# Gated linear recurrence and mixture of experts on one core: recurrences in eight halves through PSUM, and a re-ordered front

## The chip, the cores and the metric

The kernel runs on one core of a Trainium2 chip. The metric is the device time of one execution in microseconds (us). The engines are PE (TensorE, matrix products), DVE (VectorE), ACT (ScalarE), POOL (GpSimd) and SP (SyncE, which here only issues DMAs). They run side by side, each through its own list of instructions in order, and wait for one another on semaphores.

## The reference

```
xn = layernorm(x)                                  # x: 16 x 256 tokens of 128 columns
# branch 1: gated linear recurrence
xc = causal depthwise conv(xn, 4 taps) + conv_b
r, i = sigmoid(xc @ W_r.T + b_r), sigmoid(xc @ W_i.T + b_i)
a = sigmoid(log_a) ** (8 r)
h[t] = a[t] * h[t-1] + sqrt(clip(1 - a*a)) * i * xc        # along the 256 tokens of a sequence
attn = rmsnorm(h @ W_out.T) * gamma
# branch 2: mixture of 8 experts, one expert a token, 512 places an expert
e = argmax(xn @ Wr);  rank = place of the token in its expert's queue;  keep = rank < 512
y[token] = keep * p[token] * relu(xn[token] @ W1[e]) @ W2[e]
out = x + attn + y
```

## The kernel before, in words

The 4096 tokens are 32 tiles of 128 rows. Columns (transposed data) are handled in 8 halves of 512 tokens (`HT`, `NH` = 8) or 4 chunks of 1024 (`TC`, `C` = 4). A sequence is `L` = 256 tokens, so a half holds two sequences and a chunk four. The order on every engine is written by hand.

**The front.** x comes in five units (`UNITS`: 4, 4, 8, 8, 8 tiles), units 0, 2 and 4 on SP's queue and 1 and 3 on ACT's. PE transposes x by halves (`tp`, into dec), ACT copies it out (`untile`), PE computes the router's logits (`router`). DVE takes the mean and variance of each unit (`moments`), ACT the square root (`root`), DVE the reciprocal (`inverse`), and then ACT and POOL write half of the normalised tiles each (`normalise`), which SP stores to `xn_rows` in DRAM. DVE then finds each token's expert and rank in two parts (`marks`, `places`, h = 0 and 1). PE helps with running counts (`counts`) and turns the one-hot products `low_eq` and `hi_val` into a table of the tokens of each expert's places (`table_of`). DVE writes that as `idx_in` and `idx_out` (semaphore `idx_done`).

**Gathers and scatters.** From `idx_done` on, POOL issues 64 indirect DMAs, 128 rows each: for each expert 4 gathers of its tokens from `xn_rows` and 4 scatters of its results to `y_rows`. Gathers run four experts ahead. The program on POOL is gathers of experts 0 to 3, then scatter(0), gather(4), scatter(1), gather(5), ... scatter(7). scatter(e) waits until DVE has copied expert e's results out of PSUM (`evict(e)`, semaphore `y_done`).

**The experts.** For expert e PE transposes the gathered rows (`turn`), ACT copies them (`columns`, xg_hi) and DVE writes the rest (`columns_rest`, xg_lo), PE multiplies with W1 in three passes (`up`, into `hbank`), ACT applies relu (`relu`), PE multiplies with W2 (`down`, into `tb`), DVE evicts (`evict`). ACT and DVE split the next weights (`lead` writes w_hi, `weights_rest` w_lo).

**The recurrence in the experts' gaps.** The tables `PE_AT`, `ACT_AT`, `DVE_AT`, `DVE_LATE`, ... say which stages of branch 1 an engine does at expert e: `AT` before evict (DVE), relu(e+1) (ACT) or up(e+1) (PE), `AFTER` and `LATE` behind them. The first two halves of the convolution are done on PE with diagonal matrices (`conv`, `biased`), the rest on DVE (`taps`). `gates` are the two gate products with tanh. `decay` writes a, `scale` the square root, `recur(c)` multiplies inp by sca and scans chunk c, `project(n)` multiplies half n with W_out into one of three `obank`s, `squares(n)` sums its squares on ACT, `rows(n)` normalises it on DVE and adds it to x.

**The end.** When all scatters have landed, SP reads `y_rows` back in eight DMAs, DVE and ACT weigh the rows by `prob` and add x_tok, and SP and ACT store the result.

## Time and profile before

| | |
|---|---|
| median of 3 runs | 140.11 us (139.97 to 140.36) |
| profiled execution, its own time | 140.53 us |
| its span, first to last instruction | 138.7 us |
| PE busy | 106.6 us (77%) |
| DVE busy | 102.7 us (74%) |
| ACT busy | 92.9 us (67%) |
| POOL busy | 88.0 us (63%) |
| granted TensorE clock, mean | 0.927 |

The span is what the trace shows; 1.8 us of the execution lie around it. A busy share is a mean over stages: the front (to 29 us), the experts (to 121 us) and the end have different limits, so each is read by itself.

### The profile page before, as it was taken

What the parts mean: (1) busy time and instruction counts of PE and PEld (TensorE: products, weight loads), DVE (VectorE), ACT (ScalarE), POOL (GpSimd) and SP (SyncE); (2) the same over time, 40 slices, a digit from 0 to 9 for tenths busy, and PEclk for the clock granted to TensorE, in tenths of its full rate; (3) what the DMA queues carried; (4) which work ended last, traced back from release to release, by engine and by line L of the source; (5) the groups of instructions that cost most, each with busy time, mean ns of one, the idle gap of its engine ahead of it and who ended that gap; (6) DMA issues with size and microseconds to landing.
All of it is one profiled execution on the core that took longest, in us unless ns stands there. A gap on an engine that the chain in (4) does not pass through costs nothing.

```text
span 138.7 us, 2167 instructions
## 1 busy us (share of the span) xinstructions
PE 106.6 (77%) x693; PEld 90.0 (65%) x693; DVE 102.7 (74%) x238; ACT 92.9 (67%) x210; POOL 88.0 (63%) x104
## 2 busy tenths in 40 slices
PE   5789876899999999999999199999999996000000
PEld 5788774764468889779789078889798895000000
DVE  7447789848999999986531199999982969914770
ACT  2368963579578689789699948389497696403650
POOL 8936649048778778787877777898777775700000
PEclk9999999999999999999999968999999999955555
DMA  3995973793355264321613511111110111149995
GB/s 87 313 264 104 371 282 135 239 369 96 57 196 156 71 210 93 152 61 38 208 38 67 197 43 39 37 35 37 41 61 27 52 59 38 38 109 287 329 330 171
DMA packets 14346, 19.20 MB, mean 138 GB/s; under 512 B 1673, under 2 KB 10121, under 8 KB 14336
## 3 DMA queue, kind: packets, MB, share of 16 engines
q1 hardware_dynamic: 8464, 12.91, 29.8%
q0 software_dynamic: 2048, 4.13, 10.0%
q10 hardware_dynamic: 3824, 2.04, 5.5%
q8 instruction: 5, 0.08, 0.2%
q14 instruction: 5, 0.04, 0.1%
HBM read 10.76 MB, written 8.39 MB: 138 GB/s over the span
## 4 chain that ended last, share of the span: by engine, by line
PE 40%; DVE 19%; ACT 16%; DMA 11%; issue 6%; SPq 1%; POOL 1%; POOLq 1%; ACTq 0%; DVEq 0%
PE bank L579 8%; PE bank L566 5%; ACT sq L733 5%; PE bank L568 5%; PE bank L567 5%; DMA dec<-y_rows 4%; DMA x_tok<-in_x 4%; PE bank L499 4%; DVE xnT L990 3%; PE bank L521 3%; PE bank L513 2%; PE bank L523 2%; PE bank L522 2%; DVE stats L803 2%; ACT xn_tok L634 2%
## 5 line engine op out<-in xcount | busy, mean ns | idle before, releaser
L380 POOL DMA_INDIRECT xn_tok<-xn_rows,idx_in x32 | 36.9, 1153 | 14.9 <-issue 14.9
L387 POOL DMA_INDIRECT y_rows<-xn_tok,idx_out x32 | 34.6, 1081 | 10.8 <-issue 9.4
L579 PE MATMUL bank<-w_raw,h_sb 128*128 128x128 f32 x256 | 29.9, 275 | 0.0
L579 PEld LDWEIGHTS bank<-w_raw,h_sb 128*128 128x128 f32 x256 | 29.2, 192 | 0.0
L720 ACT ACTIVATE h_sb<-bank 128x512 f32<-128x512 f32 x32 | 19.2, 599 | 10.5 <-PE bank L568 8.7
L566 PE MATMUL bank<-xg_hi,w_hi 128*128 128x512 f32 x32 | 13.5, 422 | 3.5 <-DVE xg_lo L962 3.5
L568 PE MATMUL bank<-xg_hi,w_lo 128*128 128x512 f32 x32 | 13.2, 413 | 0.0
L567 PE MATMUL bank<-xg_lo,w_hi 128*128 128x512 f32 x32 | 13.1, 408 | 0.0
L356 POOL TENSOR_SCALAR xn_tok<-x_tok,rstd,nmr 128x128 f32<-128x128 f32 x16 | 8.7, 554 | 6.9 <-DVE nmr L813 6.9
L962 DVE TENSOR_TENSOR xg_lo<-bank,xg_hi 128x512 fp32r<-128x512 f32 x8 | 5.5, 687 | 9.7 <-ACT xg_hi L714 9.6
L955 DVE SCALAR_TENSOR_TENSOR xc<-xnT,par,xc 128x1020 f32<-128x1020 f32 (+2 forms) x9 | 11.5, 1278 | 0.3
L765 ACT ACTIVATE dec<-dec,prob 128x128 f32<-128x128 f32 x16 | 5.1, 390 | 8.9 <-DMA dec<-y_rows 8.9
L566 PEld LDWEIGHTS bank<-xg_hi,w_hi 128*128 128x128 f32 x32 | 6.3, 196 | 6.4 <-DVE xg_lo L962 5.1
L733 ACT ACTIVATE sq<-bank 128x128 f32<-128x128 f32 x32 | 8.8, 274 | 2.0 <-PE bank L593 1.2
L990 DVE TENSOR_TENSOR_SCAN xnT<-dec,inp 128x256 f32<-128x256 f32 x16 | 9.7, 667 | 0.0
L419 PE MATMUL bank<-w_router,dec 128*128 128x128 f32 x64 | 8.8, 280 | 0.9 <-ACT dec L639 0.9
L1012 DVE SCALAR_TENSOR_TENSOR sca<-bank,rms,gam 128x128 f32<-128x128 f32 x32 | 9.0, 345 | 0.3
L419 PEld LDWEIGHTS bank<-w_router,dec 128*128 128x128 f32 x64 | 7.8, 191 | 1.5 <-ACT dec L639 1.4
L593 PE MATMUL bank<-par,xnT 128*128 128x128 f32 x64 | 8.3, 275 | 0.0
L593 PEld LDWEIGHTS bank<-par,xnT 128*128 128x128 f32 x64 | 7.9, 192 | 0.2
L695 ACT ACTIVATE dec<-bank,half_b 128x512 f32<-128x512 f32 x8 | 5.5, 688 | 3.6 <-PE bank L523 3.1
L643 ACT ACTIVATE xnT<-bank 128x512 f32<-128x512 f32 x8 | 4.3, 601 | 4.7 <-PE bank L477 4.6
(129 smaller groups left out, 230.4 us busy)
## 6 DMA issues: line engine op xcount, KB each, us to landing
w_raw<-in_weights SPq DMA_DIRECT2D x8, 512.0 KB, 3.7
y_rows<-sca SPq DMA_DIRECT2D x4, 512.0 KB, 6.2
dec<-y_rows SPq DMA_DIRECT2D x8, 256.0 KB, 5.6
xn_rows<-xn_tok SPq DMA_DIRECT2D x3, 512.0 KB, 3.8
x_tok<-in_x SPq DMA_DIRECT2D x2, 512.0 KB, 7.5
out<-dec SPq DMA_DIRECT2D x4, 256.0 KB, 3.7
out<-dec ACTq DMA_DIRECT2D x4, 256.0 KB, 3.5
x_tok<-in_x ACTq DMA_DIRECT2D x1, 512.0 KB, 9.1
```

The lines of the kernel that those rows point to most:

```text
L380: g.indirect_dma_start(gathered[:, s * D:(s + 1) * D], None, xn_rows, bass.IndirectOffsetOnAxis(ap=idx_in[:, s:s + 1], axis=0)).then_inc(g ...
L387: g.indirect_dma_start(y_rows, bass.IndirectOffsetOnAxis(ap=idx_out[:, s:s + 1], axis=0), gathered[:, s * D:(s + 1) * D], None, bounds_che ...
L419: last = mm((bank[6], bank[2])[t // PT][:, o:o + D], xT[:, t * P:(t + 1) * P], w_router[:, :], start=True, stop=True)
L566: mm(b, w_hi[:, e % 2, w], xg_hi[:, :], start=True, stop=False)
L567: mm(b, w_hi[:, e % 2, w], xg_lo[:, :], start=False, stop=False)
L568: mm(b, w_lo[:, e % 2, w], xg_hi[:, :], start=False, stop=True).then_inc(h_mm, 1)
L579: last = mm(tile_of(e, s), h_sb[:, k * CAP + s * P:k * CAP + (s + 1) * P], w_raw[:, e, F + k * D:F + (k + 1) * D], start=(k == 0), stop=(k ...
L593: last = mm(obank[n % 3][:, i * D:(i + 1) * D], hs[:, t * P:(t + 1) * P], par[:, WO_T:WO_T + D], start=True, stop=True)
L720: a(h_sb[:, k * CAP:(k + 1) * CAP], hbank[n % 3][:, :], ACT.Relu).then_inc(h_done, 1)
L733: a(sq[:, :], obank[n % 3][:, i * D:(i + 1) * D], ACT.Square, accum_out=ssq[:, t:t + 1]).then_inc(ssq_done, 1)
L955: ins = v.scalar_tensor_tensor(dst[:, :, back:], src[:, :, 0:L - back], par[:, k:k + 1], dst[:, :, back:], ALU.mult, ALU.add)
L990: last = v.tensor_tensor_scan(hs[:, o:o + L], dec[:, o:o + L], inp[:, o:o + L], 0.0, ALU.mult, ALU.add)
```

## The change

It does these things:

1. x comes in on SP's queue alone, in the order of the units. DVE's `moments(1)` and `moments(2)` move ahead of `inverse(0)` and `inverse(2)`. ACT does `root(1)` ahead of `normalise(0)` and `untile(7)` ahead of `root(4)`. POOL writes the diagonal matrices ahead of `normalise(4)`.
2. PE does three transposes of normalised halves before the counts instead of two, and cuts the convolution of half 0 into pieces between `counts(1)` and the tables. Banks: `conv_bank` is bank 1 and 3, `xn_bank` has three banks.
3. DVE's first convolution (`taps_of_chunk(1)`) and the split of the gate weights move ahead of the probability (now a function `probability`).
4. `recur` works on halves, n = 0 to 7. Its product goes to an `obank` in PSUM (`IN_OBANK`) and the scan reads it there. Each product waits for the scan before it. `rows` writes its product back into the `obank` in place, and the sum reads it there.
5. `scale`, `recur`, `rows` and `lead` move in the tables; `evict(7)` comes ahead of rows 4. Expert 6 is put into two banks and evicted in two pieces, on which its scatters wait separately. `project(2)` now waits for recur 5, and `project(4)` for recur 7, since the scans use their banks.

```diff
-        conv_bank = [bank[7], bank[3]]
-        xn_bank = [bank[4], bank[5], bank[0], bank[1]]
+        conv_bank = [bank[1], bank[3]]
+        xn_bank = [bank[4], bank[5], bank[0]]
+        IN_OBANK = (1, 2, 2, 2, 2, 2, 1, 1)
+        SPLIT_K = ((E - 2) * KF + 2) % 3
+            if e == E - 2 and s < ST // 2:
+                return hbank[SPLIT_K][:, s * D:(s + 1) * D]
...
-        ACT_AT = {0: "decay0 gates1", 1: "gates2", 2: "gates3", 3: "scale1", 7: "squares6 squares7"}
-        ACT_AFTER = {0: "decay1", 1: "decay2", 2: "decay3 scale0", 3: "scale2 scale3", 4: "squares0 squares1",
-                     5: "squares2 squares3", 6: "squares4 squares5"}
-        DVE_AT = {0: "gated0 clip0", 1: "gated1", 2: "clip2", 3: "clip3"}
+        ACT_AT = {0: "decay0 gates1", 1: "gates2", 2: "gates3", 3: "scale0", 4: "scale2", 5: "scale3",
+                  7: "squares6 squares7"}
+        ACT_AFTER = {0: "lead2 decay1", 1: "lead3 decay2", 2: "lead4 decay3", 3: "lead5 scale1", 4: "lead6 squares0 squares1",
+                     5: "lead7 squares2 squares3", 6: "squares4 squares5"}
+        DVE_AT = {0: "gated0 clip0", 1: "gated1", 2: "clip2", 3: "clip3", 4: "recur2", 5: "recur5"}
-        DVE_LATE = {0: "taps3 split2", 1: "split3 clip1 gated2", 2: "gated3", 3: "recur0 recur1", 4: "recur2 recur3", 5: "rows0 rows1",
-                    6: "rows2 rows3 rows4", 7: "rows5 rows6 rows7"}
+        DVE_LATE = {0: "taps3 split2", 1: "split3 clip1 gated2", 2: "gated3", 3: "recur0 recur1",
+                    4: "recur3 recur4", 5: "rows0 rows1 recur6 recur7", 6: "rows2 rows3", 7: "rows4 rows5 rows6 rows7"}
...
-                if u not in ACT_UNITS:
-                    sp.dma_start(tiles(x_tok, t0, nt), tile_rows(x_rows, t0, nt)).then_inc(x_in[u], 16)
+                sp.dma_start(tiles(x_tok, t0, nt), tile_rows(x_rows, t0, nt)).then_inc(x_in[u], 16)
...
             def scatter(e):
                 for s in range(e * ST, (e + 1) * ST):
-                    pool.wait_ge(y_done, s + 1 if e == E - 1 else ST * (e + 1))
+                    if e == E - 1:
+                        pool.wait_ge(y_done, s + 1)
+                    elif e == E - 2:
+                        pool.wait_ge(y_done, (s // 2 + 1) * 2)
+                    else:
+                        pool.wait_ge(y_done, ST * (e + 1))
...
-            columns_of(0)
-            columns_of(1)
-            table_of(0)
+            for n in range(3):
+                columns_of(n)
+            conv(0, 0, 2)
             counts(1)
...
-            for n in range(2, 6):
+            table_of(0)
+            columns_of(3)
+            conv(0, 2, 3)
+            table_of(1)
+            conv(0, 3, TAPS)
+            for n in range(4, NH):
                 columns_of(n)
-            table_of(1)
-            columns_of(6)
-            columns_of(7)
-            conv(0, 0, TAPS)
             conv(1, 0, TAPS)
...
+                    if e == E - 1 and n % 3 == SPLIT_K:
+                        pe.wait_ge(y_done, ST * (E - 2) + ST // 2)
...
             def project(n):
-                pe.wait_ge(scan_done, n // 2 + 1)
+                pe.wait_ge(scan_done, {2: 6, 4: 8}.get(n, n + 1))
                 if n >= 3:
-                    pe.wait_ge(attn_done, 4 * (n - 2))
+                    pe.wait_ge(sum_done, n - 2)
...
             root(0)
             untile(0)
             untile(1)
+            root(1)
             normalise(0)
-            root(1)
...
-            for n in range(NH):
+            for n in range(4):
                 keep_columns(n)
...
             lead(0)
+            for n in range(4, NH):
+                keep_columns(n)
...
-            def recur(c):
-                dve.wait_ge(scale_done, c + 1)
-                dve.wait_ge(gated_done, c + 1)
-                for half in halves(c):
-                    v.tensor_tensor(inp[:, half], inp[:, half], sca[:, half], ALU.mult).then_inc(input_done, 1)
-                for s in range(SC):
-                    o = c * TC + s * L
-                    dve.wait_ge(input_done, 2 * c + 1 + s // 2)
-                    last = v.tensor_tensor_scan(hs[:, o:o + L], dec[:, o:o + L], inp[:, o:o + L], 0.0,
+            def recur(n):
+                cols = slice(n * HT, (n + 1) * HT)
+                given = obank[IN_OBANK[n]][:, :]
+                dve.wait_ge(scale_done, n // 2 + 1)
+                dve.wait_ge(gated_done, n // 2 + 1)
+                if n >= 1:
+                    dve.wait_ge(scan_done, n)
+                if n == 6:
+                    dve.wait_ge(sum_done, 2)
+                v.tensor_tensor(given, inp[:, cols], sca[:, cols], ALU.mult).then_inc(input_done, 1)
+                dve.wait_ge(input_done, n + 1)
+                for s in range(HT // L):
+                    o = n * HT + s * L
+                    last = v.tensor_tensor_scan(hs[:, o:o + L], dec[:, o:o + L], given[:, s * L:(s + 1) * L], 0.0,
                                                 ALU.mult, ALU.add)
...
-                    v.scalar_tensor_tensor(attn[:, t * D:(t + 1) * D], obank[n % 3][:, i * D:(i + 1) * D],
-                                           rms[:, t:t + 1], gam[:, :], ALU.mult, ALU.mult).then_inc(attn_done, 1)
+                    o = obank[n % 3][:, i * D:(i + 1) * D]
+                    v.scalar_tensor_tensor(o, o, rms[:, t:t + 1], gam[:, :], ALU.mult, ALU.mult).then_inc(attn_done, 1)
...
-                v.tensor_tensor(x_tok[:, cols], x_tok[:, cols], attn[:, cols], ALU.add).then_inc(sum_done, 1)
+                v.tensor_tensor(x_tok[:, cols], x_tok[:, cols], obank[n % 3][:, :], ALU.add).then_inc(sum_done, 1)
...
             dve.wait_ge(xnT_done, 4)
             taps_of_chunk(1)
+            split_gates()
+            probability()
             columns_rest(0)
             weights_rest(1)
-            split_gates()
             split(1)
```

How the rows stand on three engines. First PE, at the end of the router (L442 / L448 is `table_of`, L477 / L483 the transposes of normalised halves, L497 and L499 / L503 and L505 the convolution's taps, of which each half has four; L427 to L535 / L433 to L541 are counts). Before:

```order
L442 MATMUL bank<-hi_val,low_eq 128x32 x16
L427 MATMUL bank<-offset,ones 128x128
L429 MATMUL bank<-run,ones 128x128
L432 MATMUL bank<-onehot,later 128x128
L434 MATMUL bank<-run,ones 128x128
L535 MATMUL bank<-run,ones 128x8 x2
L477 MATMUL bank<-ident,xn_tok 128x128 x16
L442 MATMUL bank<-hi_val,low_eq 128x32 x16
L477 MATMUL bank<-ident,xn_tok 128x128 x8
L497 MATMUL bank<-xnT,diag 128x512
L499 MATMUL bank<-xnT,diag 128x2x255
L499 MATMUL bank<-xnT,diag 128x2x254
```

and of the change:

```order
L503 MATMUL bank<-xnT,diag 128x512
L505 MATMUL bank<-xnT,diag 128x2x255
L433 MATMUL bank<-offset,ones 128x128
L435 MATMUL bank<-run,ones 128x128
L438 MATMUL bank<-onehot,later 128x128
L440 MATMUL bank<-run,ones 128x128
L541 MATMUL bank<-run,ones 128x8 x2
L448 MATMUL bank<-hi_val,low_eq 128x32 x16
L483 MATMUL bank<-ident,xn_tok 128x128 x4
L505 MATMUL bank<-xnT,diag 128x2x254
L448 MATMUL bank<-hi_val,low_eq 128x32 x16
L505 MATMUL bank<-xnT,diag 128x2x253
```

The first two taps of half 0 now stand ahead of the counts, the third ahead of the second `table_of` and the fourth behind it; the transposes of the last four halves follow there.

DVE at experts 4 and 5 (L962 is `columns_rest`, L997 / L1002 `evict`, L986 / L991 the product of `recur` and L990 / L995 its scans, L928 / L937 `weights_rest`, L1008 / L1020 the start of `rows`). Before, from `columns_rest` of expert 5 on:

```order
L962 TENSOR_TENSOR xg_lo<-bank,xg_hi 128x512
L997 COPY xn_tok<-bank 128x512
L986 TENSOR_TENSOR inp<-inp,sca 128x512 x2
L990 SCALAR_TENSOR_TENSOR xnT<-dec,inp 128x256 x4
L986 TENSOR_TENSOR inp<-inp,sca 128x512 x2
L990 SCALAR_TENSOR_TENSOR xnT<-dec,inp 128x256 x4
L928 TENSOR_TENSOR w_lo<-w_raw,w_hi 128x512
L962 TENSOR_TENSOR xg_lo<-bank,xg_hi 128x512
L997 COPY xn_tok<-bank 128x512
L1008 RECIPROCAL rms<-rms 128x4
```

and of the change, from the same instruction:

```order
L962 TENSOR_TENSOR xg_lo<-bank,xg_hi 128x512
L991 TENSOR_TENSOR bank<-inp,sca 128x512
L995 SCALAR_TENSOR_TENSOR xnT<-dec,bank 128x256 x2
L1002 COPY xn_tok<-bank 128x512
L991 TENSOR_TENSOR bank<-inp,sca 128x512
L995 SCALAR_TENSOR_TENSOR xnT<-dec,bank 128x256 x2
L991 TENSOR_TENSOR bank<-inp,sca 128x512
L995 SCALAR_TENSOR_TENSOR xnT<-dec,bank 128x256 x2
L937 TENSOR_TENSOR w_lo<-w_raw,w_hi 128x512
L962 TENSOR_TENSOR xg_lo<-bank,xg_hi 128x512
L991 TENSOR_TENSOR bank<-inp,sca 128x512
L995 SCALAR_TENSOR_TENSOR xnT<-dec,bank 128x256 x2
```

Where four scans followed two products, now two scans follow one, with the product in a bank; one half stands ahead of each evict.

ACT around expert 4 (L725 / L735 is `scale` and its table load, L714 / L724 `columns`, L720 / L730 `relu`, L673 / L681 `lead`, L708 and L710 / L718 and L720 `decay`). Before, from the relu of expert 3 on:

```order
L720 ACTIVATE h_sb<-bank 128x512 x4
L673 ACTIVATE w_hi<-w_raw 128x512
L708 ACTIVATE dec<-dec,lna 128x1024
L710 ACTIVATE sca<-dec 128x1024
L725 ACT_TABLE_LOAD
L725 ACTIVATE sca<-sca,eps 128x1024
L714 ACTIVATE xg_hi<-bank 128x512
L725 ACTIVATE sca<-sca,eps 128x1024
L720 ACTIVATE h_sb<-bank 128x512 x4
L673 ACTIVATE w_hi<-w_raw 128x512
```

and of the change:

```order
L730 ACTIVATE h_sb<-bank 128x512 x4
L681 ACTIVATE w_hi<-w_raw 128x512
L718 ACTIVATE dec<-dec,lna 128x1024
L720 ACTIVATE sca<-dec 128x1024
L724 ACTIVATE xg_hi<-bank 128x512
L735 ACT_TABLE_LOAD
L735 ACTIVATE sca<-sca,eps 128x1024
L730 ACTIVATE h_sb<-bank 128x512 x4
L681 ACTIVATE w_hi<-w_raw 128x512
L735 ACTIVATE sca<-sca,eps 128x1024
L724 ACTIVATE xg_hi<-bank 128x512
```

`columns` of expert 4 now stands ahead of the table load and of all scales, and the other scales stand one by one between the later stages.

## Rows read from the trace of the kernel before

**Rows 1.** The page's first part: busy time by engine.
```profile
PE 106.6 (77%) x693; PEld 90.0 (65%) x693; DVE 102.7 (74%) x238; ACT 92.9 (67%) x210; POOL 88.0 (63%) x104
```
**Rows 2.** Timeline of POOL: start, length, line, operands, idle before.
```profile
29.44 1.17 POOL L380 DMA_INDIRECT xn_tok<-xn_rows,idx_in  x1 [5.49 <-issue]
...
86.43 1.40 POOL L387 DMA_INDIRECT y_rows<-xn_tok,idx_out  x1 [0.30 <-issue]
...
115.94 0.97 POOL L387 DMA_INDIRECT y_rows<-xn_tok,idx_out  x1 [1.32 <-DVE xn_tok L1002]
...
120.16 0.97 POOL L387 DMA_INDIRECT y_rows<-xn_tok,idx_out  x1 [0.30 <-issue]
```
**Rows 3.** POOL's busy time by stretch (instructions in brackets), clock, DMA.
```profile
82.00:98.00 16.00, 13.37 (x9) 0.92 0.13 37
98.00:115.00 17.00, 12.85 (x13) 1.00 0.16 49
```
**Rows 4.** Timeline of DVE, the last stage.
```profile
114.89 0.88 DVE L1002 COPY xn_tok<-bank 128x128 f32<-128x128 f32 x4
...
121.13 0.69 DVE L1016 TENSOR_TENSOR x_tok<-x_tok,sca 128x512 f32<-128x512 f32 x1
125.50 1.14 DVE L1065 SCALAR_TENSOR_TENSOR dec<-dec,prob,x_tok 128x128 f32<-128x128 f32 x4 [3.68 <-DMA dec<-y_rows]
```
**Rows 5.** The chain that ended last, merged: start, length, what.
```profile
26.83 1.44 PE bank L442 x16
...
29.15 0.86 PE bank L497 x2
...
36.84 0.63 PE bank L553 x4
...
76.14 1.28 ACT L725
...
78.58 0.49 ACT xg_hi L714
...
92.98 0.62 ACT w_hi L673
...
97.17 0.49 ACT xg_hi L714
...
98.43 0.50 PE bank L566
```
**Rows 6.** Timeline of PE: the second unit's wait, then expert 4.
```profile
7.40 0.66 PE L455 MATMUL bank<-ident,x_tok 128*128 128x128 f32 x4 [1.19 <-DMA x_tok<-in_x]
...
79.85 0.50 PE L566 MATMUL bank<-xg_hi,w_hi 128*128 128x512 f32 x1 [3.08 <-DVE xg_lo L962]
...
81.59 0.63 PE L566 MATMUL bank<-xg_hi,w_hi 128*128 128x512 f32 x1
```
**Rows 7.** Stretches of the x load: per engine, clock, DMA share, GB/s.
```profile
3.50:4.50 1.00, 1.00 (x7) 1.00 (x6) 0.06 (x1) 0.26 (x1) 1.00 (x1) 1.00 1.13 346
7.50:8.50 1.00, 1.00 (x10) 1.00 (x11) 0.65 (x2) 0.40 (x1) 0.30 (x1) 1.00 1.21 290
```
**Rows 8.** Timeline of DVE in the front.
```profile
14.88 0.29 DVE L844 TENSOR_REDUCE top<-bank 128x16 f32<-128x128 f32 x1
...
28.38 0.19 DVE L910 TENSOR_SCALAR idx_in<-bank 128x32 int32<-128x32 f32 x1 [0.21 <-PE bank L442]
```
**Rows 9.** Groups by line and form: busy, mean ns of one, idle before.
```profile
L566 PE MATMUL bank<-xg_hi,w_hi 128*128 128x512 f32 x32 | 13.5, 422 | 3.5 <-DVE xg_lo L962 3.5
L990 DVE TENSOR_TENSOR_SCAN xnT<-dec,inp 128x256 f32<-128x256 f32 x16 | 9.7, 667 | 0.0
L1012 DVE SCALAR_TENSOR_TENSOR sca<-bank,rms,gam 128x128 f32<-128x128 f32 x32 | 9.0, 345 | 0.3
L962 DVE TENSOR_TENSOR xg_lo<-bank,xg_hi 128x512 fp32r<-128x512 f32 x8 | 5.5, 687 | 9.7 <-ACT xg_hi L714 9.6
L986 DVE TENSOR_TENSOR inp<-inp,sca 128x512 f32<-128x512 f32 x8 | 5.1, 677 | 0.0
```

73 lines of the change are left out of this document (37 added, 36 removed).

## The prediction

> **What bounds the kernel now.** I read the busy times first [rows 1]. No engine is over 77% busy, so a mean share says little, and I went on to each engine's timeline. POOL's shows that from the first gather at 29.44 to the last scatter at 120.16 it issues 64 indirect DMAs one behind the other, with 0.30 between them. Its only other wait is at the 61st, the first scatter of expert 7, which stood 1.32 idle until DVE had evicted a tile [rows 2]. Of those 1.32 the usual 0.30 go off, so POOL waited 1.0 for the others and is otherwise its own bound. Its issues aren't equally long: nine of them between 82 and 98 take 13.37, which is 1.49 each; thirteen between 98 and 115 take 12.85, which is 0.99 each [rows 3]. In the slow stretch DVE does its 16 scans and 8 products of the recurrence, all of them with two inputs in SBUF; the issue at 86.43 fell wholly into scans and took 1.40 [rows 2, 9].
>
> The end hangs on POOL. Its last issue ends at 121.13; the first read-back reaches DVE at 125.50, 4.37 later, after DVE had idled 3.68 [rows 2, 4]. DVE's own last normalised row ended at 121.82 [rows 4]. So the end is bound by POOL, and DVE is 3.7 behind it as the next bound. From 125.50 to the end of the span are 13.2, which the change leaves alone.
>
> PE is the second lane. It starts the first `turn` at 36.84 [rows 5], is then full to expert 3, and stands 3.08 before `up(4)` at 79.85 [rows 6], because ACT did a table load at 76.14 and a scale ahead of xg_hi at 78.58 [rows 5]. Behind that wait TensorE fell to the lower clock level (a matmul of 0.63 in `up(4)`, where the mean of its line over all experts is 0.42) [rows 6, 9]; the stretch's granted clock is 0.92 in the mean [rows 3], a mix of the 2.4 and the 1.2 GHz level.
>
> **The front: 1.5 earlier.** The second unit of x lets PE go on at 7.40 [rows 6]. With one queue nearly alone the DMAs moved 346 GB/s, with both 290 [rows 7]. In the order of the units, 0.52 MB must be in before unit 1 is, which at 0.35 MB a us is 1.5 us of transfer, and unit 0 by itself let DVE begin about 4.6. So unit 1 is there at about 5.4 and PE goes on at 6.1, behind its own earlier work. From there I followed ACT's list, since each of DVE's `inverse` waits for a `root` on it: `marks(0)`, at 14.88 before [rows 8], comes at about 13.2, 1.7 earlier. From `marks(0)` to `idx_in` at 28.38 [rows 8] DVE has the same instructions, so all of it moves by 1.7, unless PE is late for the last table. A tap on PE takes 0.86 [rows 5], so the two early ones 1.7. They start once ACT has copied half 0, at 19.9, and end at 21.6, ahead of `counts(1)`, which needs a one-hot at 22.0: hidden. The first table (1.3, of the length of the second's 1.44 [rows 5]), four transposes, 0.44, and the third tap, 0.86, then stand ahead of the last table, which PE reaches at 25.5 where DVE would have let it begin at 26.83 − 1.7 = 25.1 [rows 5]. That costs 0.2 to 0.4 and leaves **1.5 for POOL's start**. SP's stores are all shifted with the tiles and stay hidden; POOL's diagonal matrices, 1.65, fit into its wait before `normalise(4)`.
>
> `turn(0)` at 36.84 [rows 5] needs the first four gathers. The four taps (3.4) taken out of the stretch ahead of it, less two transposed halves (0.9) put in, make PE ready at about 34.2, so it waits for the gathers, which come 1.5 earlier, at about 35.3. But DVE's taps, two SBUF inputs again, now run beside the first four gathers instead of the fifth to eighth. One issue among those got longer by 0.7; I charge 0.3 to both lanes: **PE 1.2 earlier**, POOL 1.2 net. From `turn(0)` on PE is full and keeps that.
>
> **The recurrence on POOL's lane.** The excess in the slow stretch is 9 x (1.49 − 0.99) = 4.5 [rows 3]. DVE's two-SBUF work in it is 16 scans (9.7 in all) and 8 products (5.1), 93% of the 16 us. With the product in PSUM, the scans have one SBUF input, and only the products stay: 8 x 0.68 = 5.4 of 16, 34% [rows 9]. In proportion 4.5 x (1 − 34/93) = 2.9 of the excess goes. Bounds: 0, if scans don't hold POOL up, and 4.5. The Trainium skill's page "SBUF — State Buffer" (Who interferes with whom) says that a DVE instruction with two SBUF inputs holds up a GpSimd instruction that reads SBUF, and one with at most one SBUF input doesn't; by it alone all of the scans' share would go, which is this term.
>
> The 1.0 wait at the 61st issue goes if expert 7 is evicted in time (below). POOL's lane: 121.13 − 1.2 − 2.9 − 1.0 = 116.0, and the read-back is on DVE at **120.4**.
>
> **The recurrence on DVE's, ACT's and PE's lanes.** Each half cost DVE (9.7 + 5.1)/8 = 1.85 before. Now the product drains (0.68), the scan starts behind a wait, and the second scan drains too (0.61 + 0.67): about 2.0. PSUM in place of SBUF I take at nothing: a product with one PSUM input takes 687 ns, with two in SBUF 677 [rows 9]. DVE never writes PSUM in this trace, and no scan reads it. Bounds: a little less than nothing (−0.01), and the fixed part once again, +0.23 an instruction (from 345 ns at 128 columns and 677 at 512, 0.865 a column and 0.234 fixed [rows 9]); the nearest row, 687, says nothing. The Trainium skill, "VectorE: DVE Perf Modes" (The TRN2 errata), gives PSUM sources 62 cycles more than SBUF, 65 ns by its clock; by it the path would be about 1.9 longer (29 instructions, below), an estimate from that page, where the rows show 10 ns.
>
> In times of before (the shift of 1.2 taken off last):
> - ACT: xg_hi of expert 4 moves ahead of the table load and scale, from 78.58 to 76.1 [rows 5]. DVE's part follows, `up(4)` starts at 77.4, not 79.85; it waits 0.3 for the relu behind the scale. Without the long wait I take the upper clock level. PE is at `turn(5)` at 80.5, `down(4)` to 84.5, project 0, `up(5)` 85.4 to 88.2: 4.1 ahead of before.
> - ACT then does lead6 and two `squares`. Before, these stood between 92.98 and 97.17 [rows 5]; now from 88.8 to 92.9. So xg_hi(6) is at 93.4, 4.1 ahead. DVE, with recur 0 to 4 done at 91.0, idles 1.8 for it, then writes xg_lo (94.1) and does recur 5, to 96.1. `project(2)` has waited for that since 93.1, **PE stands 3.0 again**, and `up(6)` starts at 97.0 against 98.43 [rows 5]. So 2.7 of the 4.1 are given back here.
> - DVE: evict(5) 96.8, rows 0 and 1 100.7 (one is a reciprocal, four products of 9.0/32 = 0.28 and a sum of 0.69: 1.97 with their waits [rows 4, 9]), recur 6 and 7 to 104.7, w_lo, and xg_lo(7) at 106.0. PE: `up(6)` to 99.8, turn, down(6) 104.7, project 4 (waits for recur 7) 105.6, `up(7)` 106.05 to 108.8, project 5 109.7, `down(7)` in four tiles 110.6 to 113.3. Expert 7's first eviction ends about 111.0, the last at 113.6, where the four stood from 114.89 on [rows 4].
> - rows 4 to 7 follow, 4 x 1.97: 121.5. Less the shift of 1.2, DVE is free at **120.3**.
>
> POOL's 61st issue would be due at 115.94 − 1.0 − 1.2 − 2.9 = 110.8, and the tile is evicted at 111.0 − 1.2 = 109.8: the wait goes, with 1.0 to spare. Both lanes end together: first read-back used at 120.4, against 125.50, **5.1 earlier**. Profiled: 140.53 − 5.1 = 135.4; its time is 0.42 over the median of the runs, so for these 140.11 − 5.1 = **135.0**.
>
> **The rivals.**
> - The clock falls behind the 3.0 stand at 93 as it did behind 3.08 at 76.8. The row of 0.63 is 0.2 over the mean of 0.42, with 8 of its 12 steps slow: about 1.6 for `up(6)`. PE's lane moves 1.6, DVE's end by 1.1 (the rest is in its idle time), POOL's not: 136.1. For it: the same length of wait. Chance 0.13.
> - Collisions stay: POOL's excess comes from the products or the descriptors, not the scans. POOL ends 2.9 later: 137.9. For it: issues beside the taps are mostly 1.0, though those have two SBUF inputs too. Against it: the issue wholly inside scans. Chance 0.12.
> - The front gives nothing, since PE's third tap and transposes and ACT's copies delay the tables by as much as the load gains, or one queue is no faster while the parameters share the engines. The 1.2 to 1.5 go: 136.4. Chance 0.07.
> - A premium for PSUM: a DVE instruction that reads or writes PSUM where SBUF stood takes a third of the fixed part more, 0.07. On DVE's path to the end are recur 5 to 7 (9 instructions) and rows 4 to 7 (5 each): 29, so 2.0 more, 137.0. Against it: 687 for 677 [rows 9]. Chance 0.06. The Trainium skill's page on VectorE, cited above, comes out close to this, an estimate.
> - Slower than before: the same mechanism at the upper bound. At 0.18 each the 5.1 are gone, at 0.23 it is 6.7 more, 141.7; it decides from 0.18 on. For it: no row has a DVE write to PSUM. Chance 0.05.
> - Better: all of the excess gone (4.5); then DVE's lane still holds 120.3, less at most 0.15 for each of its three late halves, 134.5: inside the first case.
>
> **How the numbers follow.** The forecast holds 0.50, with its own range from 133.0 to 136.0 (the front's 0.3 and POOL's lane by its bounds). The rivals are 0.13, 0.12, 0.07, 0.06 and 0.05, and 0.07 are two of them at once (0.02 still faster, 0.03 the same, 0.02 slower). From 133.0 to 138.0 lie the forecast and the first four rivals, with their tails cut 0.8. A measurement of this kernel tells about 0.3% (0.4 us) from no change. Faster 0.90, same 0.03, slower 0.07.
>
> **What would show it.** `idx_in` at 26.9 (27.2 or later: front wrong). POOL's first issue at 27.9; in the stretch of the recurrences a mean issue of about 1.15, not 1.49; no wait of POOL at its 61st. `up(4)` with a wait under 1; a wait of about 3 on PE before project 2, for DVE's fifth recurrence. Products of 0.68 and scans of 0.67 with PSUM operands. DVE's last row ending at 120 to 121, and an idle time before the first final instruction below 0.5 instead of 3.68. The forecast is wrong above all if the PSUM forms are longer, or if POOL's issues stay at 1.49.

## The result: 5.8 to 7.2 us faster, and the profile after

| | before | after |
|---|---|---|
| median of the runs (four each, side by side) | 140.07 us | 134.28 us (132.64, 133.29, 135.27, 135.62) |
| ratio of the undisturbed runs, 95% interval | | 0.949 [0.9445, 0.9533] |
| profiled execution, its own time | 140.53 | 132.64 |
| its span | 138.7 | 130.8 |

The ratio leaves out two of the four executions of the changed kernel (135.27 and 135.62), which are over 1.5% behind the fastest and had a lower granted clock, 0.937 and 0.924 against 0.940; by it these 140.07 us become 132.9. That is the mean of the two fastest executions, so the second measurement of the same kernel (`a_whole`, below) counts as much: 134.37 us and 0.959 [0.9514, 0.9662], which is 134.3 of 140.07. "Faster" was right in both. The forecast of 135.0 stands 0.7 above the median of the four and above the second measurement, and 2.1 above the time by the ratio, which lies 0.1 below the stated range.

The page of the changed kernel, busy times first, then POOL's two groups. They answer [rows 1]:

```profile
PE 105.0 (80%) x693; PEld 88.5 (68%) x693; DVE 103.5 (79%) x239; ACT 92.7 (71%) x210; POOL 81.4 (62%) x104
...
L381 POOL DMA_INDIRECT xn_tok<-xn_rows,idx_in x32 | 32.0, 1001 | 16.4 <-issue 16.4
L393 POOL DMA_INDIRECT y_rows<-xn_tok,idx_out x32 | 33.0, 1032 | 12.2 <-issue 9.1
```

Only POOL's busy time changed by much, by 6.6 us (PE's by 1.6), and the 64 indirect issues make up 6.4 of it: they sum to 65.06, where those of before sum to 71.44. Next POOL's timeline, against [rows 2]:

```profile
27.39 1.17 POOL L381 DMA_INDIRECT xn_tok<-xn_rows,idx_in  x1 [6.94 <-issue]
...
31.49 1.01 POOL L381 DMA_INDIRECT xn_tok<-xn_rows,idx_in  x1 [0.30 <-issue]
...
99.94 1.48 POOL L393 DMA_INDIRECT y_rows<-xn_tok,idx_out  x1 [0.30 <-issue]
104.17 0.97 POOL L393 DMA_INDIRECT y_rows<-xn_tok,idx_out  x1 [2.75 <-DVE xn_tok L1009]
...
113.12 0.97 POOL L393 DMA_INDIRECT y_rows<-xn_tok,idx_out  x1 [0.30 <-issue]
```

and its busy time by stretch, instructions in brackets, then clock, DMA share and GB/s, against [rows 3]:

```profile
75.00:98.00 23.00, 17.51 (x19) 1.00 0.17 50
98.00:115.00 17.00, 10.60 (x11) 1.00 0.14 43
```

The recurrences now lie between 76 and 102. The reader is to see two things. The stretch counts parts of issues at its ends; the seventeen issues that lie wholly between 75 and 98 take 0.99 in the mean, where the eight wholly between 82 and 98 took 1.53 before (1.49 with the parts, [rows 3]). One long one is left, 1.48 at 99.94. And POOL, which before had no wait until its 61st issue, now stands 2.75 idle until 104.17 for DVE's eviction of expert 6. With what it saved it has run ahead of its supplier.

PE's timeline, against [rows 5, 6]:

```profile
6.06 0.60 PE L461 MATMUL bank<-ident,x_tok 128*128 128x128 f32 x4
...
34.06 0.66 PE L560 MATMUL bank<-ident,xn_tok 128*128 128x128 f32 x4 [0.31 <-DMA xn_tok<-xn_rows,idx_in]
...
74.40 0.50 PE L575 MATMUL bank<-xg_hi,w_hi 128*128 128x512 f32 x1 [0.62 <-DVE xg_lo L962]
...
93.14 1.16 PE L604 MATMUL bank<-par,xnT 128*128 128x128 f32 x8 [3.00 <-DVE xnT L995]
94.05 0.47 PE L575 MATMUL bank<-xg_hi,w_hi 128*128 128x512 f32 x1
94.36 0.39 PE L576 MATMUL bank<-xg_lo,w_hi 128*128 128x512 f32 x1
```

The 3.08 ahead of `up(4)` have become 0.62, and a stand of 3.00 has appeared ahead of project 2, for DVE's half 5; the 0.39 at 94.36 says that here the clock did not fall behind it. DVE's timeline, the front and the end, against [rows 8, 4]:

```profile
13.01 0.28 DVE L856 TENSOR_REDUCE top<-bank 128x16 f32<-128x128 f32 x1
...
26.33 0.19 DVE L919 TENSOR_SCALAR idx_in<-bank 128x32 int32<-128x32 f32 x1 [0.20 <-PE bank L448]
...
118.17 0.69 DVE L1028 TENSOR_TENSOR x_tok<-x_tok,bank 128x512 f32<-128x512 f32 x1
118.77 1.13 DVE L1088 SCALAR_TENSOR_TENSOR dec<-dec,prob,x_tok 128x128 f32<-128x128 f32 x4
```

The first final instruction follows the last row with no idle time, where 3.68 stood before. It starts 6.73 earlier than the 125.50 of [rows 4]; from there to the end of the span are 12.03 instead of 13.20. That is 7.9 in all, the difference of the spans. Last the groups by form, against [rows 9]:

```profile
L995 DVE TENSOR_TENSOR_SCAN xnT<-dec,bank 128x256 f32<-128x256 f32 x16 | 10.1, 673 | 0.3
L1025 DVE SCALAR_TENSOR_TENSOR bank<-bank,rms,gam 128x128 f32<-128x128 f32 x32 | 9.1, 352 | 0.3
L991 DVE TENSOR_TENSOR bank<-inp,sca 128x512 f32<-128x512 f32 x8 | 5.6, 696 | 1.1 <-ACT sca L735 0.6
```

A scan from PSUM takes 673 ns against 667, a product into PSUM 696 against 677, a scaled row with its output in PSUM 352 against 345. The bank is not the reason for most of this: in `e3b_sbuf` below, with the same waits and the product in SBUF, they are 678 and 688.

### The profile page after: what moved, and what is told of

It reads as the page before. It is cut to its first block, busy times and chain, and to the rows that moved or that the text cites. A ratio compares the mean times of both kernels' runs of the same rounds, so it can differ in the third digit from the quotient of the medians.

```text
span 130.8 us, 2174 instructions
## 1 busy us (share of the span) xinstructions
PE 105.0 (80%) x693; PEld 88.5 (68%) x693; DVE 103.5 (79%) x239; ACT 92.7 (71%) x210; POOL 81.4 (62%) x104
## 4 chain that ended last, share of the span: by engine, by line
PE 51%; ACT 12%; DMA 10%; issue 9%; DVE 8%; POOL 5%; POOLq 1%; SPq 1%; DVEq 0%; ACTq 0%
PE bank L590 15%; PE bank L575 6%; PE bank L577 6%; PE bank L576 6%; PE bank L604 4%; DMA dec<-y_rows 4%; PE bank L527 3%; DMA xn_rows<-xn_tok 3%; PE bank L414 3%; ACT xn_tok L642 2%; POOL xn_tok L381 2%; ACT sq L743 2%; PE bank L560 2%; PE bank L529 2%; PE bank L528 2%
## 5 line engine op out<-in xcount | busy, mean ns | idle before, releaser
L381 POOL DMA_INDIRECT xn_tok<-xn_rows,idx_in x32 | 32.0, 1001 | 16.4 <-issue 16.4
L393 POOL DMA_INDIRECT y_rows<-xn_tok,idx_out x32 | 33.0, 1032 | 12.2 <-issue 9.1
L730 ACT ACTIVATE h_sb<-bank 128x512 f32<-128x512 f32 x32 | 18.9, 598 | 9.2 <-PE bank L577 7.3
L575 PE MATMUL bank<-xg_hi,w_hi 128*128 128x512 f32 x32 | 13.2, 411 | 0.6 <-DVE xg_lo L962 0.6
L577 PE MATMUL bank<-xg_hi,w_lo 128*128 128x512 f32 x32 | 12.6, 393 | 0.0
L576 PE MATMUL bank<-xg_lo,w_hi 128*128 128x512 f32 x32 | 12.5, 390 | 0.0
L962 DVE TENSOR_TENSOR xg_lo<-bank,xg_hi 128x512 fp32r<-128x512 f32 x8 | 5.5, 689 | 6.8 <-ACT xg_hi L724 6.8
L995 DVE TENSOR_TENSOR_SCAN xnT<-dec,bank 128x256 f32<-128x256 f32 x16 | 10.1, 673 | 0.3
L1025 DVE SCALAR_TENSOR_TENSOR bank<-bank,rms,gam 128x128 f32<-128x128 f32 x32 | 9.1, 352 | 0.3
```

The source lines that it names most:

```text
L381: g.indirect_dma_start(gathered[:, s * D:(s + 1) * D], None, xn_rows, bass.IndirectOffsetOnAxis(ap=idx_in[:, s:s + 1], axis=0)).then_inc(g ...
L393: g.indirect_dma_start(y_rows, bass.IndirectOffsetOnAxis(ap=idx_out[:, s:s + 1], axis=0), gathered[:, s * D:(s + 1) * D], None, bounds_che ...
L575: mm(b, w_hi[:, e % 2, w], xg_hi[:, :], start=True, stop=False)
L576: mm(b, w_hi[:, e % 2, w], xg_lo[:, :], start=False, stop=False)
L577: mm(b, w_lo[:, e % 2, w], xg_hi[:, :], start=False, stop=True).then_inc(h_mm, 1)
L730: a(h_sb[:, k * CAP:(k + 1) * CAP], hbank[n % 3][:, :], ACT.Relu).then_inc(h_done, 1)
```

## The experiments

**What they had to tell apart.** The prediction's theory, A: POOL's issues are held up by scans whose two inputs are in SBUF, and the product in PSUM frees them. Theory B: they are held up by an unbroken run of DVE instructions, and the halves, each with a wait behind its product and behind its scans, let POOL in. Beside these, what the front gave, and what the new stand of 3.00 costs.

**Four first runs.** These ran on a chip where the kernel before itself took 155.3 us (150.0 to 161.5), with extra stands of 1 to 8 us on PE and POOL; their times, 154.4 to 156.3, tell nothing apart. What their traces show of single stretches is used once, and all four kernels were run again on other chips.

`e1_front`, the front alone:

> The front of the change alone (x on one queue, DVE's, ACT's and POOL's new order of the moments, PE's first convolution in pieces, DVE's first convolution ahead of the probability), with the recurrences and the experts' stages of before. Theory A (the front is worth what the changed kernel's first turn shows, 36.84 - 34.06 = 2.8 on PE, and 2.05 on POOL's first issue): first turn at about 34.1, first gather issued at 27.4, the end 2.1 to 2.8 earlier, 137.3 to 138.0 us. Theory B (the front is worth the 1.2 to 1.5 of the prediction, the rest came from the recurrences): first turn at 35.3 or later, 138.6 to 138.9 us.

`e2_back`, the other part alone:

> The recurrences, rows, scales and expert 6's two pieces of the change alone, with the front of before. Theory A (PE's lane keeps its first turn at 36.84, POOL loses its 4.5 of excess, DVE's last row ends 0.2 before 121.8 and bounds the end, and the last stage is about 1 us shorter because the read-back has landed): the first final instruction at 121.7, 135.0 to 135.6 us. Theory B (the two halves of the change need one another): less than 2 us of gain, 138 us or more.

`e3_sbuf`, the product in SBUF:

> The changed kernel with the recurrence's product written back into inp in SBUF, as before, and read there by the scans; nothing else is changed, not even the waits. Theory A (two SBUF inputs of the scans hold up POOL's descriptor issues): POOL's issues in the stretch of the recurrences go back from about 1.0 to about 1.45 us in the mean; of that excess of 4.5 POOL's wait of 2.75 at expert 6's first scatter takes up a part, so the last scatter comes 1.5 to 2 later and the end 1 to 1.7 later, 134.0 to 134.6 us for the fast runs. Theory B (the issues are short for another reason, such as the single halves or the shifted times): POOL's mean issue stays near 1.0 and the time stays within 0.4 us of the changed kernel's fast runs (132.6 to 133.3). In both, product and scan take the same time on DVE as with PSUM within 0.02 us.

`e4_recur5`, half 5 moved ahead:

> The changed kernel with the sixth half's recurrence (recur 5) behind recur 4 at expert 4, instead of behind the residue of expert 6's columns at expert 5. Theory A (PE's 3.0 stand before project 2 is the order of DVE's list): the stand falls below 0.6, and since DVE's recur 6 and 7 then bound up(7), the end comes 1.5 to 2.2 earlier, 130.6 to 131.6 us for fast runs. Theory B (the stand is ACT's two squares ahead of xg_hi of expert 6): PE stands as long one step later, before up(6), and the time stays within 0.5 us.

Measured: 154.5, 156.28, 154.57 and 154.36 us, inconclusive. POOL's 64 issues summed to 70.5 for the front alone, and to 66.3 with the product in SBUF (`e3_sbuf`) as well as with it in PSUM (`e4_recur5`). This was the first sign that PSUM isn't needed for the gain.

**The changed kernel again, `a_whole`** (no edit).

> The changed kernel itself, unchanged, beside the experiments of this call, so that each can be set against it on the same chip. Both theories: as measured, 0.949 of before, 132 to 134 us; first gather issued at 27.4, turn(0) at about 34.1, project 2 behind a wait of about 3.0, POOL's wait ahead of expert 6's first scatter about 2.7, last normalised row ending at 118.9.

Measured: 134.37 us (133.51 to 134.89), 0.959. First gather 27.68, `turn(0)` 34.28, stand 2.99, POOL's wait 2.07, last row 119.10. The theories say the same here; it is the measure for the next three, which ran on the same chip.

**The product back in SBUF, halves and waits kept, `e3b_sbuf`.**

```diff
-                given = obank[IN_OBANK[n]][:, :]
+                given = inp[:, cols]
```

> The changed kernel with the product of each recurrence written to SBUF, where the input stands, instead of PSUM; order and halves stay. In the changed kernel's trace POOL's 64 issues sum to 65.1 us (71.4 before). Theory A (scans with two inputs in SBUF hold POOL's issues up): the issues that lie beside scans go back to 1.4 us, the sum to 68 to 70; since POOL had 2.75 us of wait ahead of expert 6's first scatter, that wait shrinks to 0 to 1 and the end moves by 1 us at most: 133 to 134.5 us. Theory B (what held them up was DVE's unbroken run of products and scans, which the halves with their waits have broken up): the sum stays at 65 to 66, the wait at 2.75, and the time is that of the changed kernel within 0.3 us. An earlier run of this kernel on a disturbed chip had a sum of 66.3, which favours B.

Measured: 134.38 us (133.09 to 135.18), 0.955 [0.9422, 0.9684]: no difference from the changed kernel. So the PSUM banks are not what made the kernel faster. The sum of the 64 issues is 65.87, against 65.06 and 65.64 in the two traces of the changed kernel. POOL's stretch, the same columns:

```profile
75.00:98.00 23.00, 17.57 (x18) 0.93 0.16 47
```

So with 16 scans from two SBUF inputs theory A expected the sum at 68 to 70, 3 to 5 us more, and 0.2 to 0.8 came. Theory B's number was 65 to 66. But single issues do tell the two kernels apart. First one that starts just behind the start of a pair of scans from SBUF, then the one at the same place in the changed kernel:

```profile
84.51 1.27 DVE L995 TENSOR_TENSOR_SCAN xnT<-dec,inp 128x256 f32<-128x256 f32 x2
84.56 1.42 POOL L393 DMA_INDIRECT y_rows<-xn_tok,idx_out  x1 [0.30 <-issue]
```
```profile
84.56 1.26 DVE L995 TENSOR_TENSOR_SCAN xnT<-dec,bank 128x256 f32<-128x256 f32 x2
84.59 0.97 POOL L393 DMA_INDIRECT y_rows<-xn_tok,idx_out  x1 [0.30 <-issue]
```

Another such couple, 0.24 and 0.23 behind the start, takes 1.20 and 0.95 (79.17 and 79.22). In the six undisturbed traces with the product in PSUM, 32 issues start within a scan with at least 0.15 of it left, and every one takes 0.94 to 1.01. So theory A holds for the single issue even with the waits; what it had wrong is how much of the excess depends on it. PE of `e3b_sbuf` shows one more thing:

```profile
93.11 1.23 PE L604 MATMUL bank<-par,xnT 128*128 128x128 f32 x8 [3.00 <-DVE xnT L995]
94.02 0.74 PE L575 MATMUL bank<-xg_hi,w_hi 128*128 128x512 f32 x1
94.56 0.63 PE L576 MATMUL bank<-xg_lo,w_hi 128*128 128x512 f32 x1
```

The same stand of 3.00 at the same place, and this time eight matmuls at 0.57 to 0.74 behind it. `turn(7)` starts at 99.33 here and at 97.79 in the changed kernel's trace: a fall of the clock costs 1.5 on PE's lane, and DVE's last row ends 1.47 later (120.33).

**Half 5 ahead of expert 5's columns, `e4b_recur5`.**

```diff
-        DVE_AT = {0: "gated0 clip0", 1: "gated1", 2: "clip2", 3: "clip3", 4: "recur2", 5: "recur5"}
+        DVE_AT = {0: "gated0 clip0", 1: "gated1", 2: "clip2", 3: "clip3", 4: "recur2"}
...
-                    4: "recur3 recur4", 5: "rows0 rows1 recur6 recur7", 6: "rows2 rows3", 7: "rows4 rows5 rows6 rows7"}
+                    4: "recur3 recur4 recur5", 5: "rows0 rows1 recur6 recur7", 6: "rows2 rows3", 7: "rows4 rows5 rows6 rows7"}
```

> The changed kernel with the sixth recurrence of DVE's list (half 5) ahead of expert 5's columns instead of behind them, so that project 2 needn't wait 3.0 us for it. Theory A (that wait delays the end): project 2 follows down(4) with a wait under 0.5, up(6) starts about 1 to 2 us earlier, expert 6 is evicted earlier, POOL's new wait of 2.75 us ahead of expert 6's first scatter shrinks to about 1 to 1.5, DVE's last row ends 0.5 to 1.5 earlier: 131.5 to 132.5 us. Theory B (DVE's own list bounds the end, in whatever order, and the wait costs nothing): DVE fills idle time ahead of expert 5's columns with it (1.9 us of idle for ACT's copy at 89.9), so the end moves by at most that, or, if ACT's copy is what is late, not at all: within 0.3 us of the changed kernel. Rival C: the long stand is what lets TensorE's granted clock fall in the executions of 135.3 to 135.6 us; without it those vanish and the median falls more than the fastest.

Measured: 131.72 us (131.27 to 132.19), 0.9395 [0.9317, 0.9473]; the changed kernel beside it 134.37. The slowest of its executions is faster than the fastest of the other. Its DVE, PE and POOL:

```profile
89.08 1.26 DVE L995 TENSOR_TENSOR_SCAN xnT<-dec,bank 128x256 f32<-128x256 f32 x2
90.26 0.67 DVE L937 TENSOR_TENSOR w_lo<-w_raw,w_hi 128x512 fp32r<-128x512 f32 x1
90.85 0.68 DVE L962 TENSOR_TENSOR xg_lo<-bank,xg_hi 128x512 fp32r<-128x512 f32 x1
```
```profile
90.40 1.16 PE L604 MATMUL bank<-par,xnT 128*128 128x128 f32 x8
91.58 0.50 PE L575 MATMUL bank<-xg_hi,w_hi 128*128 128x512 f32 x1
```
```profile
102.63 0.97 POOL L393 DMA_INDIRECT y_rows<-xn_tok,idx_out  x1 [0.86 <-DVE xn_tok L1009]
```

DVE stood 1.94 idle for ACT's xg_hi ahead of its L962 in the changed kernel; now half 5 fills that time, and L962 starts only 0.36 later (90.85 for 90.49). Project 2 follows with no stand, 2.74 earlier, `up(6)` 2.5 earlier, POOL's new wait shrinks from 2.75 to 0.86, and the last row ends at 117.31 for 118.86. Theory A of this edit is right, and the time is in its 131.5 to 132.5. The medians differ by 2.65, more than the 1.55 of the two traces. Rival C would give the rest: with no stand there, none of four executions was over 132.2, and the matmuls of `up(6)` in the trace take 0.39 to 0.50. That part is argued, not shown; against the trace of `a_whole`, the nearer one, the last row ends 1.8 earlier (119.10). This version beats both kernels.

**DVE's taps and probabilities back in their old places, `e6_taps`.**

```diff
             weights_rest(0)
+            kept = put(v.tensor_scalar(keep[:, :], hi16[:, :], float(CAP), None, ALU.is_lt))
...
             taps_of_chunk(1)
-            split_gates()
-            probability()
             columns_rest(0)
             weights_rest(1)
+            split_gates()
```

> The changed kernel with DVE's first convolution (its taps for the second chunk) and the probabilities and the split of the gate weights back in the places of before, behind the last columns of expert 0 rather than ahead of them. Theory A (the taps' place decides what the first four gathers land with): turn(0) of PE, at 34.06 in the changed kernel with 0.31 of wait for the gathers, is later by 0.3 to 1, as DVE reaches the four taps beside gathers 5 to 8, whose issues go back to 1.2 to 1.7 us; end later by 0.5 to 1.5 us. Theory B (the place costs nothing, since POOL and PE wait for other things there): turn(0) within 0.2, time within 0.3 us of the changed kernel.

Measured: 135.55 us (134.96 to 136.03), 0.9645 [0.9568, 0.9723]; the interval overlaps that of the changed kernel, so it is not settled. `turn(0)` is 0.73 later than beside it (35.01 for 34.28), but POOL's first gather was already 0.58 later (28.26 for 27.68), ahead of anything that the edit touches, and the clock fell behind its stand. So of `turn(0)` at most 0.2 is the taps' place; POOL's issues sum to 66.61, 1.0 more, and one beside the taps took 1.71 at 33.74, as theory A said.

**The kernel before with waits alone, `e7_gaps`.**

```diff
-                for half in halves(c):
+                for i, half in enumerate(halves(c)):
                     v.tensor_tensor(inp[:, half], inp[:, half], sca[:, half], ALU.mult).then_inc(input_done, 1)
-                for s in range(SC):
-                    o = c * TC + s * L
-                    dve.wait_ge(input_done, 2 * c + 1 + s // 2)
...
-                last.then_inc(scan_done, 1)
+                    dve.wait_ge(input_done, 2 * c + 1 + i)
+                    for s in range(2 * i, 2 * i + 2):
+                        o = c * TC + s * L
...
+                    last.then_inc(scan_done, 1)
+                    if i == 0:
+                        dve.wait_ge(scan_done, 2 * c + 1)
```

> The kernel before with one thing changed: in each recurrence DVE does product, its wait, two scans, and a wait for these scans, then the same for the second half, where before it did two products and four scans that overlapped each other's ends. The product stays in SBUF. Theory B (POOL's issues are held up by an unbroken run of DVE instructions and get in when DVE drains at a wait): POOL's 64 issues sum to 67 to 68.5 us instead of 71.4, no issue of 1.4 or more beside scans is left but one or two; DVE takes 0.1 to 0.2 more per half. Theory A (two SBUF inputs of the scans hold them up, however they follow each other): the sum stays at 70.5 to 72. In both the end hangs on the first eviction of expert 7, which stood ready 1.0 before POOL without the collisions, so that POOL's gain turns into wait: 139 to 141.5 us, same.

Measured: 142.01 us (141.60 to 142.51, eight runs), before 140.69, 1.0082 [1.0042, 1.0121]. The sum of the issues is 68.13 instead of 71.44. Its POOL by stretch, as [rows 3]; its DVE; then POOL beside it:

```profile
82.00:98.00 16.00, 12.34 (x13) 0.89 0.17 50
```
```profile
81.97 0.68 DVE L986 TENSOR_TENSOR inp<-inp,sca 128x512 f32<-128x512 f32 x1
82.68 1.27 DVE L990 TENSOR_TENSOR_SCAN xnT<-dec,inp 128x256 f32<-128x256 f32 x2
```
```profile
82.60 0.94 POOL L380 DMA_INDIRECT xn_tok<-xn_rows,idx_in  x1 [0.30 <-issue]
83.85 0.94 POOL L380 DMA_INDIRECT xn_tok<-xn_rows,idx_in  x1 [0.30 <-issue]
```

The product ends at 82.65 and the scans begin at 82.68: each instruction behind a wait starts when the one ahead has ended, while in an unbroken run it starts some 0.08 before. With these gaps the eleven issues wholly between 82 and 97.5 take 1.04 in the mean (one of them 1.42) beside the very products and scans in SBUF beside which eight took 1.53. The sum is theory B's, and theory A's 70.5 to 72 is excluded. But a gap doesn't let every issue in: four that start in a scan with 0.21 to 0.34 of it left still take 1.01 to 1.12. The time was expected the same and is 1.15 us longer: a half costs DVE 0.19 more (7.85 for four of them instead of 7.08), xg_lo of expert 5 is late, PE stands 2.42 at 91.14, which it had not, the clock falls behind that, and POOL's saved 3.3 turn into waits of 1.66, 3.72 and 1.90. In this trace the indices are also 0.9 late (`idx_in` at 29.29), ahead of the edit. Freeing POOL alone was worth nothing.

**The front alone, `e1b_front`, and the rest alone, `e2b_back`.** The first has the recurrences, leads, evictions and tables of before, the second has the front of before.

> The front alone (x on one queue, the first convolution in PE's gaps, DVE's taps ahead of the last columns), the recurrences, leads, evictions and rows as before. From the changed kernel's trace the front puts POOL's first issue 2.05 earlier and turn(0) 2.8 earlier. Theory: both lanes move by 2.05 and 2.8, POOL's excess beside the scans stays (sum of its issues 70 to 71.5), the end moves by 2.0 to 2.8: 137.3 to 138.2 us. Rival: the front's gain is taken up by longer issues and waits in the middle: 139 to 140.

> The other part alone: recurrences by halves through PSUM, leads of ACT, evictions of expert 6 by halves and rows in PSUM, with the front of before. If the parts add up, the 7.1 us of the whole less the front's 2.0 to 2.8 are left: 135 to 136 us. POOL's first issue at 29.4, sum of its issues 66.5 to 68 (the early long ones beside DVE's taps stay), PE stands 3.0 before project 2. Rival: the whole gains only because DVE's list and POOL's start moved together, and this part alone gives 3 or less: 137 or more.

Measured: front 137.85 us, 0.980 [0.9709, 0.9885], 2.9 us; the rest 136.28 us, 0.967 [0.9592, 0.9744], 4.7 us. Together 7.5, where the whole gave 7.2 and, the second time, 5.8: within their intervals the parts add up, and neither needs the other. The front's 2% is at the edge of what counts as a difference. In the front alone the first issue is at 28.39 and `turn(0)` at 35.10, both 1.0 later than expected; against `e7_gaps`, which has the front of before and ran on the same chip, they are 1.96 and 2.66 earlier. POOL's issues sum to 69.1, below the 70 to 71.5 expected, and stay long beside the unbroken runs:

```profile
80.00:95.00 15.00, 12.32 (x9) 0.91 0.13 39
```

With the rest alone they sum to 66.7, the first gather is at 29.49, and PE stands 2.99 ahead of project 2, all as expected. Here the gain is POOL's alone: DVE ends its last row at 121.96, no earlier than before (121.82), but POOL's last issue ends 3.94 earlier (117.19), and the first final instruction starts at 121.88 and no longer at 125.50. Which of the rest's parts is needed for that (ACT's new order, the halves, expert 6 in two pieces, expert 7 ahead of rows 4) was not taken apart.

**x on two queues again, all else changed, `e5_twoq`.**

```diff
+        ACT_UNITS = (1, 3)
...
             for u, (t0, nt) in enumerate(UNITS):
-                sp.dma_start(tiles(x_tok, t0, nt), tile_rows(x_rows, t0, nt)).then_inc(x_in[u], 16)
+                if u not in ACT_UNITS:
+                    sp.dma_start(tiles(x_tok, t0, nt), tile_rows(x_rows, t0, nt)).then_inc(x_in[u], 16)
...
+            for u in ACT_UNITS:
+                act.dma_start(tiles(x_tok, t0, nt), tile_rows(x_rows, t0, nt)).then_inc(x_in[u], 16)
```

> The changed kernel with x on two queues again (units 1 and 3 from ACT's), all else as changed. Theory A (one queue brings the second unit 1.3 us earlier and everything up to the indices with it): PE's second columns wait till 7.2 to 7.5, marks(0) is at 14.5 to 14.9 instead of 13.0, POOL's first issue 1.2 to 2.0 later, the end 1 to 2 us later: 134.5 to 136 us. Theory B (the order of DVE's and PE's work ahead of the indices made the gain): POOL's first issue within 0.5 of 27.5, time within 0.5 us of the changed kernel.

Measured: 137.81 us (136.13 to 138.03), 0.976 [0.9678, 0.9849], 2.5 us more than the changed kernel by the ratios. Its DVE in the front:

```profile
7.59 0.76 DVE L818 BATCH_NORM_STATS2 stats<-x_tok 128x6 f32<-128x256 f32 x2 [0.93 <-DMA x_tok<-in_x]
...
16.02 0.28 DVE L863 TENSOR_REDUCE top<-bank 128x16 f32<-128x128 f32 x1
...
29.75 0.19 DVE L926 TENSOR_SCALAR idx_in<-bank 128x32 int32<-128x32 f32 x1 [0.20 <-PE bank L452]
```

PE waits 1.27 for the second unit, until 7.61, as theory A said, and 0.1 later than it said. But `marks(0)` is not at 14.5 to 14.9, it is at 16.02, 3.0 later than in the changed kernel and 1.1 later than before [rows 8], and the time is above theory A's 134.5 to 136. Two things are mixed here. In the new order DVE's `moments(1)` stands ahead of `inverse(0)`, so its wait for the second unit, until 7.59, now holds up the first unit as well. And behind PE's wait its rows run slow in this trace: four transposes take 1.11 where before has 0.66, the eight router products behind them 1.91 for 1.06. `e7_gaps`, the old order with two queues, has the same slow rows (1.12, 1.92), and there the marks are at

```profile
15.81 0.28 DVE L844 TENSOR_REDUCE top<-bank 128x16 f32<-128x128 f32 x1
```

So with two queues the new order costs 0.2 at `marks(0)` and brings nothing; 0.9 of the 1.1 is PE's slow rows. One queue with the old order was not run.

**An unbroken run for halves 0 and 1, from PSUM (`e8_pair_psum`) and from SBUF (`e9_pair_sbuf`).** Both are the changed kernel with `pair`: two products, then four scans, as before.

```diff
-        DVE_LATE = {0: "taps3 split2", 1: "split3 clip1 gated2", 2: "gated3", 3: "recur0 recur1",
+        DVE_LATE = {0: "taps3 split2", 1: "split3 clip1 gated2", 2: "gated3", 3: "pair0",
...
+                for n in (2 * c, 2 * c + 1):
+                    v.tensor_tensor(given, inp[:, cols], sca[:, cols], ALU.mult).then_inc(input_done, 1)
+                for n in (2 * c, 2 * c + 1):
+                    dve.wait_ge(input_done, n + 1)
...
```

> The changed kernel with halves 0 and 1 of the recurrence in one unbroken run of DVE: two products into PSUM, then four scans, as the kernel before orders them (the rest by halves, with waits). In the changed kernel the five issues of POOL between 74.1 and 80.5, beside these halves, take 0.95 to 1.00 each. Theory A (PSUM frees POOL whatever the order): they stay at 0.95 to 1.1, apart from one beside the products. Theory B (only a drain of DVE lets POOL in, PSUM does nothing): one or two of them take 1.4 to 2.0, as in the run from SBUF beside it. The end moves by less than 0.5 us in both, since only two halves are touched.

> The same unbroken run of two products and four scans for halves 0 and 1, the products in SBUF. Both theories expect long issues of POOL here: one to three of the five take 1.4 to 2.6 us, as in the kernel before beside its recurrences (1.47, 1.39, 1.40, 2.63, 1.46, 1.46). If none is longer than 1.1, the place in the program matters and not the run of instructions, and neither theory holds.

One execution each, on the chip where before takes 159 us; only the stretch is read. DVE and POOL of the first, PSUM:

```profile
93.60 1.29 DVE L1005 TENSOR_TENSOR bank<-inp,sca 128x512 f32<-128x512 f32 x2
94.80 2.41 DVE L1012 TENSOR_TENSOR_SCAN xnT<-dec,bank 128x256 f32<-128x256 f32 x4
```
```profile
94.49 1.28 POOL L393 DMA_INDIRECT y_rows<-xn_tok,idx_out  x1 [2.95 <-DVE xn_tok L1019]
96.07 0.99 POOL L393 DMA_INDIRECT y_rows<-xn_tok,idx_out  x1 [0.30 <-issue]
```

and of the second, SBUF:

```profile
95.84 1.28 DVE L1005 TENSOR_TENSOR inp<-inp,sca 128x512 f32<-128x512 f32 x2
97.04 2.43 DVE L1012 TENSOR_TENSOR_SCAN xnT<-dec,inp 128x256 f32<-128x256 f32 x4
```
```profile
96.73 1.27 POOL L393 DMA_INDIRECT y_rows<-xn_tok,idx_out  x1 [2.89 <-DVE xn_tok L1019]
98.30 1.39 POOL L393 DMA_INDIRECT y_rows<-xn_tok,idx_out  x1 [0.30 <-issue]
```

The two are alike to 0.02 up to the issue that lies wholly beside scans: 0.99 beside scans from PSUM, 1.39 from SBUF. That is theory A for an unbroken run, with one issue of each kind; the 1.39 and 1.40 of the issues at 83.43 and 86.43 before are of the SBUF kind too. The first run's expectation had nothing over 1.1 apart from one beside the products, and there is one more: its next issue, 97.37, takes 1.28 beside `weights_rest`, which also has two SBUF inputs, where the second run's takes 0.97. So the three issues sum to 3.55 and 3.63.

**What the rows say together.** In the ten undisturbed traces 104 of POOL's issues, the first of each trace aside, take 1.10 or more. 93 of them start while DVE is in an instruction with two SBUF inputs, and end 0.75 to 0.89 behind its end, 0.83 in the mean (instructions inside a merged row taken as evenly spaced). The 1.48 at 99.94 in the changed kernel is one: the product beside it ends at 100.59, the issue at 101.42. So the single DVE instruction holds the issue, not the unbroken run, and how long depends on how much of it is left. It also explains why DVE's taps look harmless, with two SBUF inputs as well: at 30.18, 31.49 and 32.80 in the changed kernel issues start 0.17 to 0.19 before a tap ends, and take 1.00 to 1.01.

Why then do waits help? This is worked out from rows, not tested. In the kernel before, an issue once held starts its successor 0.83 + 0.30 = 1.13 behind the release, and scans follow one another every 0.59, so two of them take 1.18: the next issue starts again near the start of a scan. Those at 92.86, 94.63 and 96.39 stand within 0.07 of such a start and wait for nearly all of it. The waits move DVE's starts against POOL's, and more issues then meet the end of an instruction. The 2.63 before, and the 2.60 in `e1b_front`, held through more than one instruction, stay unexplained.

## Why the prediction was right in its course and short in its size

- **The front, 1.5 for POOL.** PE went on at 6.06 (said 6.1), `marks(0)` was at 13.01 (13.2), `idx_in` at 26.33 (26.9), POOL's first issue at 27.39 (27.9). The steps held; 2.05 came for 1.5, because the last table was not late by the 0.2 to 0.4 that I charged for PE's taps, and `marks(0)` gained 0.2 more. That the new order brings nothing with two queues (`e5_twoq`) was not in it. Its reading of the transfer was off: it took 346 GB/s for one queue and 290 for two, but with one queue the same stretches show 344 and 289. Unit 1 is earlier because it no longer shares that rate with unit 2, not because the rate is higher.
- **PE 1.2 earlier: the term that was mis-sized most.** It measured 2.8 (34.06 for 36.84). The failed step is "it waits for the gathers, which come 1.5 earlier, at about 35.3": it took 36.84 for the time at which the gathers had landed, but that row [rows 5] has no wait for them; PE came to it straight from its own work. In the trace of after, PE does wait, 0.31, and from the fourth gather's issue to `turn(0)` are 2.57 (31.49 to 34.06), where before they are 3.13. So 0.56 of the old time was PE's, not the gathers'. Another 0.55 is the index time above, 0.3 the charge for a collision that didn't come (all of the first sixteen issues but the first take 0.94 to 1.02), 0.2 the shorter issues up to the fourth. DVE's lane carries this term to the end, and that lane set the end: POOL's last issue ended at 114.09, which with the 4.37 of before makes 118.5, and DVE was free at 118.86.
- **POOL's excess, 4.5 of which 2.9 goes.** Right in what holds an issue up, wrong in "in proportion", and so in size. The issues lost 6.4 in all: 1.7 in the first sixteen (17.74 to 16.05), which the sum didn't have, and 4.7 in the nine of the slow stretch (the 39th to 47th, 13.72 to 8.98), which is about the stated upper bound of 4.5. "In proportion" shared the excess out by DVE's busy time, but what an issue loses depends on where in an instruction it starts. So the waits that came with the halves do it nearly alone: the same nine sum to 9.32 in `e7_gaps` and 9.64 in `e3b_sbuf`, all inputs in SBUF. The Trainium skill's page "SBUF — State Buffer" (Who interferes with whom), which I drew on, is borne out by the 32 issues inside scans from PSUM, 0.94 to 1.01, and by the 0.99 against the 1.39. Its rule alone would have scans from two SBUF inputs hold POOL up with gaps between them too, and the 1.42 at 84.56 in `e3b_sbuf` agrees. But the error cost nothing: 121.13 − 2.05 (start) − 6.4 (issues) − 1.0 (61st issue) would be 111.7, and the wait for expert 6's first eviction, 2.45 above the usual 0.30, makes it 114.1 (measured 114.09). This wait was not foreseen; the prediction asked only for expert 7's.
- **`up(4)` and the new stand of PE.** `up(4)` waited 0.62 (said under 1), project 2 3.00 (said 3.0), for the named reason. Taken with the shift of 2.8, DVE's last row would be at 121.5 − 2.8 = 118.7; measured 118.86. This part of the sum was right to 0.2.
- **PSUM at nothing.** Right. 6 to 19 ns more for an instruction, over the 29 on the path 0.2 at most, and part of it comes with the waits (688 and 678 ns from SBUF in `e3b_sbuf`). The Trainium skill, "VectorE: DVE Perf Modes" (The TRN2 errata), would have it 65 ns by its clock; no row here shows that. The two rivals on a PSUM premium, one of them the slower case, fall.
- **"The change leaves alone" the 13.2 of the tail.** It was 12.0. In ten traces of this study it lies between 11.7 and 13.2, also in `e7_gaps` (12.1), which changes nothing there; the execution before was the longest of them. It is 1.2 of the 7.9 and no gain of the change.
- **The clock's rival, 0.13.** It happens, from execution to execution: behind nine stands of 2.99 to 3.08 in nine traces the clock fell in five (before, `e1b_front`, `e3b_sbuf`, `e5_twoq`, `e6_taps`) and held in four (after, `a_whole`, `e2b_back`, and the first stand of `e7_gaps`). Its price on PE's lane was 1.5, as reckoned, but DVE's and POOL's ends moved by as much (1.47 and 1.46 in `e3b_sbuf`), where 1.1 and nothing were reckoned: POOL now waits for expert 6, which comes off that lane. Whether it makes the executions of 135.3 and 135.6 is open. The profiled execution of `e3b_sbuf`, with the fall, took 133.74 at a clock of 0.934, so one such fall is too little for them, and 0.937 is hardly lower than 0.940.
- **The sum.** 5.1 were forecast for the profiled execution and 7.9 came: 1.6 from PE's earlier start, 1.2 from the tail, 0.1 from rounding. The profiled execution was the fastest of its four; in that of `a_whole` the last row ends at 119.10 and the tail is 12.7, which makes 7.0.

## What to carry to other kernels

A time at which an instruction started is the time of what it waited for only if its row shows a wait; otherwise it is a bound, and a term built on it is too small. If an engine off the path gets faster, ask for every supplier that it has, not for the one that was late before: POOL's 6.4 were cut to the next eviction, and freed by themselves (`e7_gaps`) they bought nothing. A stand of PE for work that another engine could have done in its own idle time is worth a look at that engine's list first: moving half 5 by one place was worth 2.6 us, where the whole change gave 5.8 beside it.

## What the hardware did that I had not expected

An indirect DMA's issue on POOL takes 0.94 to 1.01 beside a scan with one input in PSUM. If it starts within a DVE instruction with two inputs in SBUF, it ends some 0.83 behind that instruction's end, and so takes up to 1.5 beside products and scans (twice 2.6, unexplained) and 1.71 beside a tap; an issue that starts at the same moment as the instruction can also take 0.97 (100.10 in `a_whole`). And in the front a small difference in time decides who is held up. In the changed kernel DVE's `hi` and `lo` take 0.17 and 0.18 while POOL's four normalisations beside them take 2.99; in `e6_taps`, with the same instructions, it is the other way round:

```profile
17.47 2.99 POOL L357 TENSOR_SCALAR xn_tok<-x_tok,rstd,nmr 128x128 f32<-128x128 f32 x4 [0.67 <-DVE nmr L821]
```
```profile
17.95 1.75 POOL L357 TENSOR_SCALAR xn_tok<-x_tok,rstd,nmr 128x128 f32<-128x128 f32 x4 [0.68 <-DVE nmr L821]
```
```profile
18.50 0.35 DVE L885 TENSOR_SCALAR hi<-rank 128x16 f16<-128x16 f32 x1
18.88 0.39 DVE L886 SCALAR_TENSOR_TENSOR lo<-rank,hi 128x16 f16<-128x16 f32 x1
```

The first row is the changed kernel's, the three others are those of `e6_taps`. The Trainium skill's page cited above says that what issues first keeps the ports and the other waits; these rows agree in that the loser changes. It puts 0.4 on the path to the indices, and so to the end, or doesn't, from one execution to the next.
